# One matmul of the recurrence moved ahead of the closing matmul of the first half

## The reference

```
# layer 0 (all 512 time steps at once)
mid = gelu(x @ base_down + (x @ a2) @ b2.T);  x = x + (x + mid @ base_up.T + (mid @ b1) @ a1.T)
# layer 1
xW = x @ Wx + b                                 # for all time steps at once
def step(prev_h, xw_t):
    next_h = tanh(xw_t + prev_h @ Wh)           # 4 x 256 by 256 x 256
    return next_h, next_h                       # 512 steps, each needs the one before
x = x + hs
```

## Time and profile before

| | before |
|---|---|
| runs, us | 568.85, 568.97, 566.21 (median 568.85) |
| profiled execution, us | 569.51 |
| its span, us | 567.6 |
| mean granted clock, share of full | 0.986 |
| PE busy (share of the span) | 510.9 us (90%), 14200 matmuls |
| PE weight loads | 429.1 us (76%), 14200 |
| DVE busy | 287.8 us (51%) |
| ACT busy | 173.9 us (31%) |
| POOL busy | 21.6 us (4%) |
| DMA, mean | 28 GB/s |

### The profile page before, as it was taken

How to read it: one execution, slowest core, us unless ns; L and a number is a source line. 1 busy time by engine, 2 the same in 40 slices (tenths; PEclk the granted TensorE clock), 3 DMA queues, 4 the chain that set the end, 5 groups by cost and what they waited for, 6 DMA issues and landing times.

```text
span 567.6 us, 31977 instructions
## 1 busy us (share of the span) xinstructions
PE 510.9 (90%) x14200; PEld 429.1 (76%) x14200; DVE 287.8 (51%) x2214; ACT 173.9 (31%) x1128; POOL 21.6 (4%) x33
## 2 busy tenths in 40 slices
PE   4979989999999999999999999999999999999995
PEld 4334458888888888888888888888888888888884
DVE  2142355555555555555555555555555555555553
ACT  3021113333333333333333333333333333333322
POOL 1039100000000000000000000000000000000000
PEclk9978989999999999999999999999999999999999
DMA  7950000000000000000000000000000000000000
GB/s 259 387 190 0 0 3 4 4 13 5 13 4 13 4 14 4 13 5 10 8 3 14 3 14 3 14 3 14 3 14 3 13 5 14 3 11 6 6 13 12
DMA packets 11216, 15.99 MB, mean 28 GB/s; under 512 B 1587, under 2 KB 6978, under 8 KB 11074
## 3 DMA queue, kind: packets, MB, share of 16 engines
q1 hardware_dynamic: 11078, 13.95, 7.4%
HBM read 11.85 MB, written 2.10 MB: 25 GB/s over the span
## 4 chain that ended last, share of the span: by engine, by line
PE 82%; ACT 8%; issue 3%; SPq 3%; DMA 3%; DVE 0%; DVEq 0%
PE bank L653 66%; ACT w_sb L358 8%; PE bank L633 7%; PE bank L589 3%; DMA w_sb<-in_L_cond_W 3%; PE bank L601 2%; SPq L227 2%; PE bank L642 1%; PE bank L628 1%; PE bank L571 1%; PE bank L578 1%; PE bank L515 0%; PE bank L554 0%; ACT xT L315 0%; DVE x2T L446 0%
## 5 line engine op out<-in xcount | busy, mean ns | idle before, releaser
L653 PE MATMUL bank<-w_sb,whp 128*128 128x52 bf16 x6132 | 244.2, 186 | 38.7 <-ACT w_sb L358 38.0
L653 PEld LDWEIGHTS bank<-w_sb,whp 128*128 128x128 bf16 x6132 | 188.5, 96 | 86.8 <-ACT w_sb L358 64.5
L479 DVE TENSOR_TENSOR r_ring<-w_sb 128x4 f32<-128x4 f32 x1022 | 136.6, 164 | 220.9 <-ACT w_sb L358 218.5
L358 ACT ACTIVATE w_sb<-bank 128x4 f32<-128x4 f32 x1024 | 142.2, 174 | 324.7 <-PE bank L653 324.7
L653 PE MATMUL bank<-r_ring,whp 128*128 128x52 bf16 x4096 | 220.7, 186 | 0.0
L653 PEld LDWEIGHTS bank<-r_ring,whp 128*128 128x128 bf16 x4096 | 174.7, 96 | 0.0
L653 PE MATMUL bank<-l_ring,whp 128*128 128x52 bf16 (+1 forms) x2048 | 157.5, 178 | 0.0
L484 DVE TENSOR_TENSOR l_ring<-r_ring 128x4 bf16<-128x4 f32 x1024 | 135.9, 162 | 0.0
L653 PEld LDWEIGHTS bank<-l_ring,whp 128*128 128x128 bf16 x2048 | 122.3, 96 | 0.0
L633 PE MATMUL bank<-xp,wxp 128*128 128x32 bf16 x1536 | 76.2, 176 | 0.0
L633 PEld LDWEIGHTS bank<-xp,wxp 128*128 128x128 bf16 x1536 | 56.2, 95 | 0.0
(11 more groups left out here) (84 smaller groups left out, 147.6 us busy)
## 6 DMA issues: line engine op xcount, KB each, us to landing
w_sb<-in_L_cond_W SPq DMA_DIRECT2D x8, 1024.0 KB, 14.0
x_sb<-in_x SPq DMA_DIRECT2D x4, 512.0 KB, 9.6
out<-o_sb SPq DMA_DIRECT2D x64, 32.0 KB, 1.6
w_sb<-in_L_cond_W SPq DMA_DIRECT2D x1, 256.0 KB
up_sb<-in_L_cond_base_up SPq DMA_DIRECT2D x1, 256.0 KB, 3.1
down_sb<-in_L_cond_base_down SPq DMA_DIRECT2D x1, 256.0 KB, 11.1
wh_sb<-in_L_cond_Wh SPq DMA_DIRECT2D x1, 256.0 KB
wx_sb<-in_L_cond_Wx SPq DMA_DIRECT2D x1, 256.0 KB
```

What stands on the lines that cost most here:

```text
L358: nc.scalar.activation(h_ring[:, m, slot(pair, s), 0:B], zt, ACT.Tanh).then_inc(h_ready, 1)
L479: nc.vector.tensor_tensor(r_ring[:, k, q, 0:B], state_before(pair, s, k)[:, 0:B], state_hi_before(pair, s, k)[:, 0:B], ALU.subtract).then_ ...
L653: return nc.tensor.matmul(zbank(p, q, m)[:, col0:col0 + n], whp[part][:, k, P * m:P * (m + 1)], rhs[:, 0:n], start=False, stop=stop, skip_ ...
```

## The change

Product 23, which multiplies weight part 0 with l of half 0 for the new half 1, now stands directly behind product 19, which does the same for the new half 0, and ahead of the wait for l1. So closing product 0 is the 21st of a step and has three behind it, where it was the 20th with four behind it. No instruction is added or removed, no operand and no wait is altered, and the lists of ScalarE and VectorE are the same.

```diff
                     pe.wait_ge(l_ready, done + 1)
-                    product(0, 0, 0, l_ring[:, 0, q, :])
+                    for m in range(K2):
+                        product(0, 0, m, l_ring[:, 0, q, :])
                     pe.wait_ge(l_ready, done + 2)
                     product(0, 1, 0, l_ring[:, 1, q, :], stop=True).then_inc(z_ready, 1)
                     for part in range(2):
                         product(part, 1, 1, r_hi[:, 1, q, :])
-                    product(0, 0, 1, l_ring[:, 0, q, :])
                     product(0, 1, 1, l_ring[:, 1, q, :], stop=True).then_inc(z_ready, 1)
```

## The result

The changed kernel took 574.87 us (median of 4 runs, 573.06 to 575.93), the kernel before 568.91 us (median of 4, 566.21 to 569.32). The ratio is 1.0107 with a 95% interval of 1.0083 to 1.013: slower by 6 us, with 4.7 to 7.4 us inside the interval. Measured again beside the later experiments, the two stood at 574.81 and 568.58 us, ratio 1.0114 (1.0095 to 1.0132).

A forecast was written before the change was run, and what follows sets the result against it. Two nearly equal loops bound the step, the one over VectorE setting it at 0.942 us. The other grows 0.009 per step x 511 = +4.6 us, on the 568.85 us median: 573.5 us, range 570.3 to 577.0.

The forecast's parts named there:

- The wait for l1 inside "busy": TensorE waits about 0.02 us for l1 before closing product 0's load, hidden because product 19 is still in the array.
- Loop B: Closing product 0, closing product 1, tanh 1, r1, l1, back to closing product 0: 0.942 us, setting the step before.
- Loop A: Tanh 0 over 20 products in a row back to tanh 0; gains a product, loses the wait: +0.009 us per step.
- way by starts: Estimate from instruction starts: tanh 0 comes 0.244 behind product 19 before and 0.254 after, +0.010 us per step.
- way by ends: Estimate from closing product 0's recorded end: 0.207 behind product 19's start before, 0.214 after, +0.007 us per step.
- recovered wait: Part of the moved product's 0.025 us won back as closing product 0 no longer waits for l1's load.
- the sum written out for loop B: 0.115 + 0.204 + 0.174 + 0.03 + 0.164 + 0.034 + 0.164 + 0.057, together 0.942 us.
- The rule on VectorE's pipe: Skill's rule that VectorE's next operation waits until the pipe empties, so r1 no nearer r0 than 0.16; R2 brings nothing.
- R2: Loop B was all that counted: the step follows it from 0.942 to 0.92, -11.2 us, 557.6 us; chance 0.04.
- R1: The wait swallows the product: ScalarE's start goes with the weight load, +0.002 per step, +1 us, 569.9 us; chance 0.15.
- R3: No wait recovered: the wait for l1 reappears at the new place, full 0.025 paid, +12.8 us, 581.7 us; chance 0.05.
- R4: TensorE's clock falls to 1.2 GHz in steps without input products, +32 us, 606 us; chance 0.03.

The follow-up runs named there:

- 19 products: Kernel before with one product (weight part 1, r of half 0) moved behind closing product 0, so 19 ahead and five behind: 580.54 us, ratio 1.0214.
- wide l1: VectorE's l1 computed over 52 columns instead of 4, in both kernels: kernel before 592.99 us (ratio 1.0443), changed kernel 580.46 us (ratio 1.0229).
- 22 products: Changed kernel with one more product (weight part 0, r of half 1) moved ahead of the wait for l1: 587.38 us, ratio 1.0347.

## Why the prediction was right

*The wait for l1 inside "busy".* Right, and shown by taking it out: 6 us in the kernel before, nothing in the changed one. The chain of waits gave VectorE 0% in both the earlier trace rows, although it set every step before.

*Loop B is the longer one before.* Right: all 50 ns of a slower l1 show, and one product more between the closing ones costs 12 us.

*Loop A, +0.009.* The direction and mechanism are right, the size was low: 0.0116 measured (0.0112 in the second profile). I took a middle between 0.007 from the recorded ends and 0.010 from the starts. The way by starts was nearly right. In the means of the traces closing product 0 starts 0.4983 behind product 1 before and 0.5199 after, 0.0216 later, where I had 0.021. Tanh 0 follows that start by 0.2142 before and by 0.2042 after, so 0.0100 comes back, where I had 0.011. The way by ends had 0.014 there, the difference of the recorded durations; so the recorded end of a product that waited says too much. The term of the sum that was mis-sized is the recovered wait: I had 0.016 (0.025 less 0.009), and taking the wait out gave 0.0134.

A part of the 0.0016 by which the way by starts is still short is that I had read the distance of products from a single step and taken it for all, and the steps of the changed kernel are not all alike. Its timeline of ScalarE, three steps in each piece:

```profile
309.76 0.25 ACT L358 ACTIVATE w_sb<-bank 128x4 f32<-128x4 f32 x2 [0.70 <-PE bank L653]
...
312.63 0.25 ACT L358 ACTIVATE w_sb<-bank 128x4 f32<-128x4 f32 x2 [0.52 <-PE bank L653]
...
314.54 0.25 ACT L358 ACTIVATE w_sb<-bank 128x4 f32<-128x4 f32 x2 [0.70 <-PE bank L653]
...
317.39 0.25 ACT L358 ACTIVATE w_sb<-bank 128x4 f32<-128x4 f32 x2 [0.70 <-PE bank L653]
```

The first three steps take 2.87, the last three 2.85: 0.957 and 0.950 each. The difference goes with the place of a step among the 16 that repeat. By place, the mean step of the changed kernel goes from 0.9487 to 0.9558, and that of the kernel before without the wait for l1 from 0.9233 to 0.9339. With 19 products, where closing product 0 is held 0.07 in every step, it goes only from 0.9659 to 0.9675. So a wait for l1 that is long enough covers such a difference, as it comes to an end at the same time anyway. The short wait of the kernel before covers a part (0.9375 to 0.9450), and in the changed kernel nothing covers it. What spaces the products a little wider in some steps I did not test, and it stays open.

*Loop B gets 0.022 shorter and is no longer the limit.* Right in both: tanh 1 follows by 0.08, and with the wide l1, where it is the limit, it is 12.5 us per 511 steps, 0.024, shorter. But the 0.92 does not follow from the sum written out for loop B: with 0.075 in place of 0.115 that sum gives 0.902. Where this loop is the limit, closing product 0 is held, and the two closing products are 0.089 apart and not 0.075. The loop is then 0.942 less 0.025, 0.917, near the 0.92 that I took from l1's coming 0.02 earlier.

*The rule on VectorE's pipe.* As I gave it, r1 couldn't have come nearer to r0 than the 0.16 of its duration, and it came within 0.08 (a pair of 0.24). I had left out how the passage goes on: in the section The DRAIN you can't avoid of "VectorE: DVE Perf Modes", the Trainium skill adds that a next operation that isn't held starts earlier. With that the trace agrees. What it disagrees with is my shortened rule, and it stays right that the rule took nothing from R2's chance.

*The rivals.* R1 (nothing to pay) and R2 (faster) fall with the measured 1.0107. R3 (full 0.025) is what the second moved product costs, when no wait is left to fill. R2's mechanism was real and waits behind a condition: by an estimate from these figures it decides once l1 is 0.012 later (loop B of the changed kernel is 0.967 - 0.050 = 0.917, loop A 0.953, and before it is 0.942: the two kernels are level where 0.942 plus the delay is 0.953). The wide l1, 0.050 later, is well beyond that point. I had put the point at 21 products in a row being shorter than loop B, which comes to the same. R4 (a fall of the clock) didn't happen: the granted clock was 1.00 from 88 to 568 us.

*The time.* 573.5 us was forecast, 574.87 measured. Of the 1.4 us, 0.0026 x 511 = 1.3 us is the size of the term. The change forecast, +4.6 us, lies at the lower edge of the interval, 4.7 to 7.4 us.

## What to carry to other kernels

An engine that waits while an earlier matmul is still in the array counts as busy, and the chain of waits then names the wrong owner of the loop. Look at the distance between weight loads and at the duration of instructions of one form: two values where one is expected are a wait. When moving work across a hand-over between engines, write out every loop that runs through it: here one loop got 0.025 longer and another 0.024 shorter, and by the estimate above a VectorE chain 0.012 longer would have been the point from which the move pays; with one 0.050 longer it saved 12.5 us.

## What the runs showed of the hardware that I had not expected

- A weight load with a fulfilled wait in front of it costs nothing, even with 0.03 us to spare (0.15 for three loads, one of them behind a wait; the mean step is 0.9529 with and without that wait).
- Tanh instructions of ScalarE can start 0.08 apart and subtractions of VectorE too, at durations of 0.17 and 0.16. With 22 products, where the closing products are 0.050 apart, tanh 1 still follows tanh 0 by 0.071 and r1 follows r0 by 0.080. Hand-overs are alike in all kernels: 0.05 from the end of a tanh or of l1 to the weight load that waited for it.
- A matmul that had to wait for its weights is recorded 14 ns longer than one in flow (178 against 164 ns for 4 columns), and tanh starts 0.215 behind its start, where it starts 0.204 behind one in flow.
- The stretch at 1.2 GHz at the start of the loop differs between executions: the changed kernel had 5 slow steps in one profile and 2 in the other.
